# A graph network on one core: three products and the dots read a PSUM bank that only VectorE touches

## The reference

```python
edge_emb = edge_attr_full @ ew.T + eb
xw = x @ W
xj = xw[src].reshape(-1, H, D) + edge_emb.reshape(-1, H, D)
xi = xw[dst].reshape(-1, H, D)
alpha = einsum('ehd,hd->eh', xi, att_i) + einsum('ehd,hd->eh', xj, att_j)
alpha = leaky_relu(alpha, NEG_SLOPE)
ea = exp(alpha - segment_max(alpha, dst)[dst])
alpha = ea / (segment_sum(ea, dst)[dst] + EPS)
aggr = segment_sum(xj * alpha[..., None], dst)
return aggr.mean(axis=1) + b
```

## Time and profile before

| what | value |
|---|---|
| median of 3 runs | 3343.92 us (3342.73 to 3345.37) |
| profiled execution, its own time | 3336.89 us |
| span of the profiled execution | 3335.0 us, 48,601 instructions |
| busy: PE, DVE, POOL, ACT | 72 %, 61 %, 65 %, 20 % |
| mean granted TensorE clock | 0.543 |

### The profile page before, as it was taken

One profiled execution on the slowest core, in us unless ns is written; L12 is line 12 of the kernel. 1 busy time (PEld: TensorE's weight loads), 2 busy tenths in 40 slices (PEclk: granted clock), 3 DMA queues, 4 the chain that ended last, 5 costly groups with the idle time before them and its releaser, 6 DMA issues.

```text
span 3335.0 us, 48601 instructions
## 1 busy us (share of the span) xinstructions
PE 2402.9 (72%) x13595; PEld 1979.9 (59%) x13595; DVE 2021.6 (61%) x6441; ACT 669.5 (20%) x3102; POOL 2172.8 (65%) x2357
## 2 busy tenths in 40 slices
PE   6879955777675677668477777747777685777668
PEld 6669924566564566556366565636556573556557
DVE  8965464665565565656655665755665574665557
ACT  0048921111114111110411111131111122111112
POOL 0047737777755777774677777377777737777772
PEclk9555555555557555555755555575555566555556
DMA  3211112222221222221222222122222212222221
GB/s 100 102 66 68 46 55 59 60 61 58 63 48 43 58 63 58 58 64 40 50 63 58 58 67 56 33 59 61 58 60 64 56 35 57 60 60 58 58 55 50
DMA packets 114123, 195.78 MB, mean 59 GB/s; under 512 B 39898, under 2 KB 77273, under 8 KB 113865
## 3 DMA queue, kind: packets, MB, share of 16 engines
q0 software_dynamic: 62560, 130.25, 17.4%
q1 hardware_dynamic: 51304, 62.42, 5.9%
HBM read 180.86 MB, written 11.67 MB: 58 GB/s over the span
## 4 chain that ended last, share of the span: by engine, by line
POOL 30%; DVE 28%; PE 22%; issue 13%; DMA 4%; DVEq 2%; ACT 1%; POOLq 0%; ACTq 0%
POOL ring L510 28%; PE bank L745 10%; PE bank L747 5%; DMA ring<-table,srci 4%; DVE acc L1208 2%; PE bank L718 2%; DVE into L1149 2%; PE bank L741 2%; DVE prod L1072 2%; DVE ring L847 2%; DVE lanes L1135 2%; DVE fwd L1156 1%; POOL ring L491 1%; PE bank L783 1%; DVEq L1016 1%
## 5 line engine op out<-in xcount | busy, mean ns | idle before, releaser
L510 POOL DMA_INDIRECT ring<-table,srci x1955 | 1903.9, 974 | 633.1 <-issue 571.4
L745 PE MATMUL bank<-pw,ring 128*128 128x48 f32 x3910 | 1216.9, 411 | 0.0
L745 PEld LDWEIGHTS bank<-pw,ring 128*128 128x128 f32 x3910 | 1009.1, 316 | 103.8 <-issue 23.9
L741 PE MATMUL bank<-zeros 128*128 128x288 bf16 x490 | 209.6, 428 | 622.0 <-DVE pw L1167 622.0
L747 PE MATMUL bank<-onehot,est 128*36 128x24 f32 x3910 | 619.1, 246 | 0.0
L747 PEld LDWEIGHTS bank<-onehot,est 128*36 128x36 f32 x3910 | 382.6, 150 | 177.5
L586 ACT ACTIVATE dd<-dd 128x66 f32<-128x66 f32 x75 | 19.4, 258 | 2152.2 <-DVE dd L1160 2152.2
L741 PEld LDWEIGHTS bank<-zeros 128*128 128x128 bf16 x490 | 54.3, 111 | 665.3 <-DVE pw L1167 630.7
L1111 DVE TENSOR_TENSOR alpha<-alpha,ring 128x56 f32<-128x56 f32 (+7 forms) x75 | 18.1, 241 | 702.6 <-DMA ring<-table,srci 702.4
L1208 DVE TENSOR_TENSOR acc<-acc,bank 128x288 f32 x490 | 222.4, 454 | 301.7 <-PE bank L747 183.0
L580 ACT COPY ai_win<-ai_rows 128x48 f32 x1955 | 309.1, 228 | 58.0 <-issue 22.7
(11 more groups left out here) (214 smaller groups left out, 2676.1 us busy)
## 6 DMA issues: line engine op xcount, KB each, us to landing
ring<-table,srci POOLq DMA_INDIRECT x1955
ai_rows<-lo_dram SPq DMA_DIRECT2D x28, 896.0 KB, 4.3
at<-in_attr SPq DMA_DIRECT2D x65, 224.0 KB, 2.5
table<-ring SPq DMA_DIRECT2D x15, 390.0 KB, 3.6
table<-ring SPq DMA_DIRECT2D x5, 325.0 KB, 3.3
result<-ring SPq DMA_DIRECT2D x24, 64.0 KB
x_mid<-ring SPq DMA_DIRECT2D x3, 384.0 KB, 2.7
table<-ring SPq DMA_DIRECT2D x5, 130.0 KB, 2.3
```

Source lines behind the costliest of these rows:

```text
L510: nc.gpsimd.indirect_dma_start(out=ring[:, slot(t), :], out_offset=None, in_=table, in_offset=bass.IndirectOffsetOnAxis(ap=srci[:, t:t + 1 ...
L741: nc.tensor.matmul(total, zeros[:, 0:P], zeros[:, :], start=True, stop=False, skip_group_check=True)
L745: nc.tensor.matmul(wide[:, 0:H, at_k], ring[:, slot(t), 0:D], pw[:, g % DEEP, k, :, :], start=False, stop=False, skip_group_check=True)
```

## The change

Bank 7 is taken out of the transposes at the start of a layer, which now use bank 6 alone. Three views of bank 7 are declared: `dot_row` (the two attention rows of the dots), `probs` (the transposed probabilities, whose SBUF tensor is gone) and `v16` (the 16 edge weights of each head). Only VectorE reads or writes the bank within the layers. The dots read `dot_row`, filled by a copy per layer behind chunk 10; the product with the edge weights reads `v16`, filled by a copy at the head of the layer; the product with the edge vectors and the product with the one-hot matrix read `probs`. The two instructions of L1088 become one, and so do the two of L1182.

```diff
-        probs = sb("probs", [P, H, QB])
...
+        dot_row = bank[7][:, 0:H * D].rearrange("p (h f) -> p h f", h=H)
+        probs = bank[7][:, H * D:H * D + H * QB].rearrange("p (h k) -> p h k", h=H)
+        v16 = bank[7][:, H * (D + QB):H * (D + QB + FA)].rearrange("p (h f) -> p h f", h=H)
...
-                                   bank[6 + q % 2][:, 0:(j1 - j0) * P].rearrange("p (j n) -> p j n", n=P)).then_inc(tr_sb, 1)
+                                   bank[6][:, 0:(j1 - j0) * P].rearrange("p (j n) -> p j n", n=P)).then_inc(tr_sb, 1)
...
-                if q >= 2:
-                    pe.wait_ge(tr_sb, NQ * layer + q - 1)
+                if q >= 1:
+                    pe.wait_ge(tr_sb, NQ * layer + q)
...
-                    nc.tensor.transpose(bank[6 + q % 2][:, o:o + P], xt[:, j, 0:D], identf[:, :]).then_inc(tr_ps, 1)
+                    nc.tensor.transpose(bank[6][:, o:o + P], xt[:, j, 0:D], identf[:, :]).then_inc(tr_ps, 1)
...
-            v.wait_ge(lay_w, 16 * 5)
+            def layer_rows(layer):
+                v.wait_ge(lay_w, 16 * 5 * (layer + 1))
+                link(V.tensor_copy(dot_row, vrow[:, :, :]))
+
+            layer_rows(0)
...
-                V.tensor_tensor_reduce(out=dump[:, d % NDUMP, :], in0=xt[:, j, 0:D], in1=vrow[:, h, :], scale=1.0,
+                V.tensor_tensor_reduce(out=dump[:, d % NDUMP, :], in0=xt[:, j, 0:D], in1=dot_row[:, h, :], scale=1.0,
...
-                    for h in range(H):
-                        ins = V.scalar_tensor_tensor(out=pr[:, h, :, :], in0=at[:, gc % NAT, 0:k, :], scalar=1.0,
-                                                     in1=v17[:, layer, h, 0:FA].unsqueeze(1).broadcast_to((P, k, FA)),
-                                                     op0=ALU.mult, op1=ALU.mult)
-                    link(ins)
+                    link(V.tensor_tensor(pr, at[:, gc % NAT, 0:k, :].unsqueeze(1).broadcast_to((P, H, k, FA)),
+                                         v16.unsqueeze(2).broadcast_to((P, H, k, FA)), ALU.mult))
...
-                                est[:, c % 2, k:k + n, HF:HF + H].unsqueeze(3).broadcast_to((P, n, H, WIN)), ALU.mult)\
+                                probs[:, :, k:k + n].rearrange("p h k -> p k h").unsqueeze(3).broadcast_to((P, n, H, WIN)),
+                                ALU.mult)\
...
-                link(V.transpose(probs[:, :, :], dd[:, 0:H * QB].rearrange("p (h e) -> p h e", h=H)))
+                link(V.transpose(probs, dd[:, 0:H * QB].rearrange("p (h e) -> p h e", h=H)))
...
-                for h in range(H):
-                    ins = V.scalar_tensor_tensor(out=es[:, :, h * FA:(h + 1) * FA], in0=at[:, gc % NAT, 0:k, :], scalar=1.0,
-                                                 in1=probs[:, h, 0:k].unsqueeze(2).broadcast_to((P, k, FA)),
-                                                 op0=ALU.mult, op1=ALU.mult)
-                ins.then_inc(est_ready, 1)
+                V.tensor_tensor(es[:, :, 0:HF].rearrange("p k (h f) -> p k h f", h=H),
+                                at[:, gc % NAT, 0:k, :].unsqueeze(2).broadcast_to((P, k, H, FA)),
+                                pr.unsqueeze(3).broadcast_to((P, k, H, FA)), ALU.mult).then_inc(est_ready, 1)
...
+                V.tensor_copy(v16, v17[:, layer, :, 0:FA])
...
                             weight_columns(layer + 1)
+                            layer_rows(layer + 1)
...
-                else:
-                    v.wait_ge(lay_w, 16 * 5 * (layer + 2))
```

## The result

| | before | with the change |
|---|---|---|
| median of 4 runs each | 3344.14 us (3342.73 to 3345.37) | 3296.34 us (3294.06 to 3297.70) |
| profiled execution, its own time | 3336.89 us | 3294.06 us |
| span of the profiled execution | 3335.0 us | 3292.3 us |

The ratio is 0.9857, with a 95 % interval of 0.9839 to 0.9874: 47.8 us less between the medians, 42.7 us less between the spans. The forecast was 40.8 us less.

A forecast was written before the change was run, and what follows sets the result against it. POOL's gathers set the pace, with 58.4 us of excess from VectorE holds, and VectorE at layer ends. -40.0 + 11.5 - 12.3 = -40.8 us gives 3303 us on the median, own range 3281 to 3315, full range 3281 to 3333.

The forecast's parts named there:

- The forecast case: Whole kernel: shorter gathers and dots take off 40.8 us, to 3303 us on the median; chance 0.72.
- Products off the shared operand: Gathers under L1182, L1167 and L1088: with one SBUF operand left, holds of 17.4, 15.2 and 7.4 us go, -40.0 us.
- What the freed gathers meet next: Gathers under the window product L1095: at a random phase it holds 27.8 us instead of 16.3, +11.5 us.
- Dots: Layer ends: 44 dots held 0.28 us each beside POOL's sum of self terms lose those holds, -12.3 us.
- Price of a PSUM operand: VectorE's dots and products reading a bank: 0 extra, after L1208; at L940's rate each dot would cost 0.087 us more.
- Transposes into one bank, copies: Mainly layer starts: at most 9 us of waits, hidden by VectorE's 15.00 us wait for gathers; copies covered too, 0.
- B: Bank operands are slow, at L940's rate, with dots over 0.40 us: 3333 us; chance 0.13.
- C: Any two-tensor VectorE instruction holds POOL wherever the operand lies, merged products longer: +25 us, 3369 us; chance 0.05.
- D: Gathers are hidden, PE's sums set the pace and only the dots pay: -12, 3332 us; chance 0.05.

The follow-up runs named there:

- run 4: The changed kernel with the two merged products split into pairs again, each half reading the bank: 3299.95 us, ratio 0.9864.
- run 3: The kernel before with the pairs of L1088 and L1182 merged into one instruction each, operands left in SBUF: 3387.65 us, ratio 1.0126.
- run 1: The changed kernel with the dots reading `vrow` in SBUF again and the copy left out: 3310.32 us, ratio 0.9896.
- run 2: The kernel before with only `dot_row`, its copy and one bank for the transposes, products as before: 3334.58 us, ratio 0.9967.
- run 7: The kernel before with only the transposes put in one bank, waiting for the quad just before: 3340.34 us, ratio 1.0001.
- run 5: The changed kernel without the window product (L1098), so its output is not the reference's: 3262.82 us, ratio 0.9769.
- run 6: The changed kernel with the windows in banks 4 to 6, their product in three instructions, and the sums on three banks: 3267.13 us, ratio 0.9783.

## Why the prediction was right

The forecast case came: 3296.34 us against 3303, inside the case's own range of 3281 to 3315. Its steps one by one:

- **Products off the shared operand (-40.0).** Right in mechanism and place. The gathers that start under the three products are free of holds in the profile after; run 4 shows that it is the operand, run 3 that it is not the form, run 1 that it comes without the dots.
- **What the freed gathers meet next (+11.5).** Right in sign; the mean at a random phase was 27.8 us for the window product, and it measured 25.5. Net for the gathers -30.6 instead of -28.5. That the size came so near is luck, for the phase is not random, and "nothing ties the new phase down" was wrong. With the change the next gather starts 0.90 to 1.05 us behind the pair's start in 41 of 65 chunks; before, it was 0.45 to 0.60 us in 34 and 1.20 to 1.35 us in 17. The holds repeat accordingly: 16.3, 18.7 and 18.1 us in the three kernels whose products lie as before (before, runs 2 and 7), 25.5, 23.4 and 23.8 us where they are off the shared operand (the change, runs 1 and 4), 33.1 us where they are merged in SBUF (run 3). What ties the phase was not tested; VectorE starts 65 of its chunks when a gather lands, which could do it.
- **Dots (-12.3).** 44 long dots became none; the four stretches shrank by 13.3 us in the profiled executions, and by itself this part was worth 11.4 us between medians (run 2). The prediction did not see that the same meeting, 0.01 us later, costs POOL instead of VectorE (run 1).
- **Price of a PSUM operand (0).** Dots 338 ns in the median against 342. L1170 takes 346 ns where L1167 took 352; a merged product takes 1080 to 1087 ns, and the slope had said 1098. Run 3 has the same product wholly in SBUF: 1084 to 1095 ns. So L940's rate does not carry over to these forms. The 62 further cycles that the Trainium skill gives for PSUM ("VectorE: DVE Perf Modes", section on the TRN2 errata) do not show in them either; the measurement decides. What did grow, off the path, were instructions with one source: the transpose into the bank from 237 to 252 ns, the copy out of it from 197 to 217 ns.
- **Transposes into one bank, copies (0).** Run 7: no difference within 0.1 %. The size behind it was near as well. The prediction had the first two quads pulled apart by 0.6 us and ACT's wait, 1.3 us together; the stretch shown grew by 1.5 us, those of the four other layers by 0.03 us at most, and in run 7 the five grew by some 6 us in all. The cover of 15.00 us took it, and 13.31 us of it are left.

**The rivals.** B (a slow operand) asked for dots over 0.40 us; they take 0.34. C (any two-tensor instruction holds POOL) asked for gathers over 0.95 us under the merged products; there are none in the bank, and in SBUF there are up to 1.84 us. So C named a real price for the wrong condition. D (the gathers hidden anyway) falls with runs 1, 5 and 6, in which the time goes down with the gathers, by 35.6 us and by more. The clock is no rival either. The mean granted TensorE clock was 0.603 in the profiled execution with the change and 0.543 before, but of the ten runs of the kernel before on the chip of runs 1 to 4, those at 0.603 and 0.604 take 3345.07 to 3347.61 us and those at 0.542 to 0.544 take 3344.24 to 3346.49.

**What stays open.** The medians moved 47.8 us and the profiled executions 42.7. The profiled execution lies below the median of its kernel's runs by 7.2 us before, 2.3 with the change, 8.5, 8.0, 5.2 and 4.0 us in runs 1 to 4, 0.5 and 0.6 us in runs 5 and 7, and not at all in run 6. The holds do not sort these, for run 7 has all of them. The chip would: runs 1 to 4 were measured on one, runs 5 to 7 on another. Why it should is open. The bank operand of L1170 was not tried by itself.

## What to carry to other kernels

Where POOL's indirect DMAs set the pace, look for gathers above the median and at what VectorE runs when they start: moving one operand of a two-operand instruction into a spare PSUM bank frees POOL; it cost these products and dots nothing. Do not merge such instructions while both operands are in SBUF, since the longer one holds longer; and count on the holders that stay to catch part of what is freed. How much depends on the phase, which here was neither random nor predicted: the mean over phases gave 27.8 us, and the line held 16.3 to 33.1 us. Follow the chain to its end: after three of the four holders, the last one was worth another 25 us of gathers.

## What the hardware showed that was not expected

- A line that nobody edits can double its cost by phase: the window product's holds were 16.3 us before, 25.5 with the change and 33.1 in run 3, at the same 0.85 us an instruction.
- The hold goes both ways. When a dot and POOL's sum both have two operands in SBUF, a sum that starts up to 0.030 us behind the dot leaves the dot at 0.62 us, and one that starts 0.032 to 0.041 us behind it takes 0.63 us itself (run 1).
- ACT's copies of 48 elements take 197 ns into a PSUM bank (run 6), against 228 ns into SBUF in the kernel before and with the change.
- The excess can be taken out almost whole: with the last two-SBUF product gone the longest of 1955 gathers is 1.14 us, where it was 1.546.
